# A graph network's second layer: ScalarE fetches one tile of rows in every 16 chunks, as SyncE does, in place of one in every 32

## The reference, cut to what matters

```python
h = jnp.maximum(_layernorm(x, axis=-1), 0.0)
H = jnp.einsum('ni,rio->rno', h, W)          # 8 relations
msg = (H[etype, src] + b[etype]) * norm
out = jax.ops.segment_sum(msg, dst, num_segments=h.shape[0])
x = x + jax.nn.relu(out)
```

## Time and profile before

| | us |
|---|---|
| median of 3 runs | 11777.57 (11773.84 to 11794.78) |
| the profiled execution | 11662.24 |
| its span, first to last instruction | 11659.8 |
| PE busy in the span | 7838.2 (67%) |
| POOL busy | 5846.3 (50%) |
| DVE busy | 4276.2 (37%) |
| ACT busy | 2363.0 (20%) |

### The profile page before, as it was taken

One profiled execution on the slowest core, in us unless ns is written; L12 is line 12 of the kernel. 1 busy time (PEld: TensorE's weight loads), 2 busy tenths in 40 slices (PEclk: granted clock), 3 DMA queues, 4 the chain that ended last, 5 costly groups with the idle time before them and its releaser, 6 DMA issues.

```text
span 11659.8 us, 215368 instructions
## 1 busy us (share of the span) xinstructions
PE 7838.2 (67%) x52954; PEld 6037.6 (52%) x52954; DVE 4276.2 (37%) x15012; ACT 2363.0 (20%) x7307; POOL 5846.3 (50%) x6213
## 2 busy tenths in 40 slices
PE   6777777777777777776555655655565555655555
PEld 5655566565665566565444444444444444444444
DVE  4333333333333333334333333333333333333333
ACT  4333333333333333334000000000000000000000
POOL 3555555555555555554444444444444444444444
PEclk8888888888888888888776777767767776777777
DMA  4222222222222222222111111111111111111111
GB/s 105 64 64 63 63 64 63 63 64 64 63 64 64 63 63 64 62 64 76 35 34 34 35 35 35 36 35 34 35 35 34 35 35 34 36 35 35 35 35 52
DMA packets 630303, 585.31 MB, mean 50 GB/s; under 512 B 306227, under 2 KB 505147, under 8 KB 629228
## 3 DMA queue, kind: packets, MB, share of 16 engines
q0 software_dynamic: 197856, 251.86, 9.9%
q1 hardware_dynamic: 422268, 325.27, 9.7%
q10 hardware_dynamic: 9600, 1.60, 0.1%
HBM read 558.88 MB, written 19.27 MB: 50 GB/s over the span
## 4 chain that ended last, share of the span: by engine, by line
SPq 31%; issue 21%; DVE 0%; PE 0%; DMA 0%; ACT 0%; DVEq 0%
SPq L548 26%; SPq L543 4%; SPq L448 1%; SPq L538 0%; SPq L555 0%; DVE res L1057 0%; SPq L414 0%; SPq L354 0%; PE bank L1222 0%; PE bank L1209 0%; DMA h_tab<-h_place 0%; PE bank L1255 0%; SPq L564 0%; DMA h_place<-in_src_t 0%; ACT h_place L660 0%
## 5 line engine op out<-in xcount | busy, mean ns | idle before, releaser
L617 POOL DMA_INDIRECT rows_place<-h_tab,idx x3055 | 2881.8, 943 | 3237.7 <-DMA idx<-in_src_t 1871.4
L617 POOL DMA_INDIRECT shared<-p_tab,idx x3128 | 2950.0, 943 | 2472.7 <-remote 992.1
L1209 PE MATMUL bank<-shared,rows_place 128*128 128x256 f32 x6110 | 2155.8, 508 | 902.4 <-DMA rows_place<-h_tab,idx 609.7
L1021 DVE SCALAR_TENSOR_TENSOR shared<-bank,key,late 128x256 f32<-128x256 f32 x3128 | 1280.3, 476 | 2932.8 <-remote 1843.2
L1209 PEld LDWEIGHTS bank<-shared,rows_place 128*128 128x128 f32 x6110 | 1490.7, 255 | 1286.0 <-DMA rows_place<-h_tab,idx 629.1
L1115 PE MATMUL bank<-h_sb,w_tile 128*128 128x128 f32 x6256 | 1079.3, 325 | 892.8 <-DVE h_sb L932 874.4
L1115 PEld LDWEIGHTS bank<-h_sb,w_tile 128*128 128x128 f32 x6256 | 909.8, 224 | 1105.0 <-DVE h_sb L932 1095.1
L775 ACT ACTIVATE h_place<-bank 128x256 f32<-128x256 f32 x782 | 298.7, 383 | 5773.2 <-remote 3342.2
L1222 PE MATMUL bank<-h_place,w_rel_sb 128*128 128x64 f32 x6256 | 915.2, 297 | 332.1 <-issue 331.4
L1134 PE MATMUL bank<-wn_half,h_sb 128*128 128x128 f32 x6256 | 1078.3, 326 | 0.0
L1222 PEld LDWEIGHTS bank<-h_place,w_rel_sb 128*128 128x128 f32 x6256 | 844.1, 212 | 348.6 <-issue 323.3
(11 more groups left out here) (94 smaller groups left out, 7034.4 us busy)
## 6 DMA issues: line engine op xcount, KB each, us to landing
rows_place<-in_dst_c SPq DMA_DIRECT2D x782, 192.0 KB
h_place<-h_tab SPq DMA_DIRECT2D x6272, 0.5 KB
shared<-in_edge_cols SPq DMA_DIRECT2D x782, 128.0 KB
shared<-p_tab,idx POOLq DMA_INDIRECT x3128
h_place<-h_tab ACTq DMA_DIRECT2D x3072, 0.5 KB
rows_place<-h_tab,idx POOLq DMA_INDIRECT x3055
qr_f<-qr_tab SPq DMA_DIRECT2D x782, 36.0 KB
idx<-in_src_t SPq DMA_DIRECT2D x393, 8.0 KB, 1.7
```

Source lines behind the costliest of these rows:

```text
L617: pool.indirect_dma_start(out=rows_of[s][:, t, :], out_offset=None, in_=table, in_offset=bass.IndirectOffsetOnAxis(ap=idx[k][:, s * TC + t ...
L1021: ins = dve.scalar_tensor_tensor(out=hot_rel[u % 2][:, t, :], in0=ps_key, scalar=key[k][:, n * TC + t:n * TC + t + 1], in1=w_f[:, ds(c.i * ...
L1209: pe.matmul(bank[s][:, 0:RW], there, hot_rel[s % 2][:, t, :], start=(t == 0), stop=(t == TC - 1))
```

## The change

ACT now fetches a tile of every superchunk, as SP does: SP fetches tile 0 of chunk 13 and ACT tile 1 of the same chunk. Both take 8 rows in each chunk's step. ACT begins two steps earlier than SP (`lead` 2), so that its last 8 rows are issued in its step of chunk 11 and SP's in the step of chunk 13. The number of ACT's tiles goes from 24 to 49 and of its rows from 3072 to 6272, and POOL gathers 3030 tiles in place of 3055. Chunk 15 is gathered whole. One load of 256 numbers by SP in step 5 brings both lists of a superchunk; ACT's own loads of lists are gone. ACT waits for that load in its step of chunk 12, and before its first copy of the layer it waits for the first list and issues 32 rows. SP issues the first list load once the last use of its place in the buffer has been stored, and waits for the other stores behind it. At chunk 13 PE waits for two semaphores, those of SP's rows and of ACT's.

```diff
-    ACT_ROWS = 5
-    ACT_FED_AT = SUP - 1
@@
-        fed_rows = h[2]
-        act_fed_rows = h[3][:, 2, :]
-        act_fed_ids = h[3][0:1, 3, :].bitcast(i32)
-        fed_ids = [h[3].rearrange("p j d -> p (j d)")[0:1, k * P:(k + 1) * P].bitcast(i32) for k in range(2)]
+        fed_rows = h[2][:, 0:4, :].rearrange("p (k f) d -> p k f d", f=2)
+        fed_ids = [h[3].rearrange("p j d -> p (j d)")[0:1, 2 * k * P:2 * (k + 1) * P].bitcast(i32) for k in range(2)]
@@
+        def feed(eng, f, lone, piece, landed):
+
+            _, at = nc.values_load_multi_w_load_instructions(
+                fed_ids[lone.half][0:1, f * P + piece * FED_ROWS:f * P + (piece + 1) * FED_ROWS], engines=(eng.engine,),
+                min_val=0, max_val=NPAD - 1, skip_runtime_bounds_check_because="a source node's number is below the number of nodes")
+            for k, row in enumerate(at):
+                p = piece * FED_ROWS + k
+                eng.dma_start(fed_rows[p:p + 1, lone.half, f, :], h_tab[ds(row, 1), :]).then_inc(landed[lone.half], 16)
+
+        def feed_step(eng, f, lead, u, lone, after, landed):
+
+            first = FED_AT - lead - SUP + 1
+            if u - first < SUP:
+                feed(eng, f, lone, u - first, landed)
+            elif after:
+                if u == first + SUP:
+                    eng.wait_ge(fed_ids_landed, 16 * after.ids_turn + 16)
+                    hold(eng)
+                feed(eng, f, after, u - first - SUP, landed)
+
+        def feed_first(eng, f, lead, m, landed):
+
+            eng.wait_ge(fed_ids_landed, 16 * Lone(m, 0, 0).ids_turn + 16)
+            hold(eng)
+            for piece in range(SUP - 1 - FED_AT + lead):
+                feed(eng, f, Lone(m, 0, 0), piece, landed)
@@
             def load_ids(lone):
-                sp.dma_start(fed_ids[lone.half], src_t[:, ds((lone.k * SUP + FED_AT) * TC, 1)].rearrange("p o -> o p"),
+                sp.dma_start(fed_ids[lone.half], src_t[:, ds((lone.k * SUP + FED_AT) * TC, 2)].rearrange("p o -> o p"),
@@
+                    feed_step(sp, 0, 0, u, lone, after, sp_row_landed)
@@
-                gather(c, k, two, h_tab, rows, scattered, idx1_landed, rows_landed, range(u == FED_AT or act_fed(u, lone), TC))
+                gather(c, k, two, h_tab, rows, scattered, idx1_landed, rows_landed, range(2 if u == FED_AT else 0, TC))
@@
             def copy_sums(c, u, k, two, lone, after):
...
+                feed_step(act, 1, 2, u, lone, after, act_row_landed)
@@
             with act.Fori(0, passes) as m:
+                feed_first(act, 1, 2, m, act_row_landed)
                 superchunks(act, m, copy_sums)
@@
                 if u == FED_AT:
-                    pe.wait_ge(fed_row_landed[lone.half], 16 * P * lone.turn + 16 * P)
-                if act_fed(u, lone):
-                    pe.wait_ge(act_row_landed, 16 * P * lone.act_turn + 16 * P)
+                    pe.wait_ge(sp_row_landed[lone.half], 16 * P * lone.turn + 16 * P)
+                    pe.wait_ge(act_row_landed[lone.half], 16 * P * lone.turn + 16 * P)
@@
-                    if u == FED_AT and t == 0:
-                        there = fed_rows[:, lone.half, :]
-                    if act_fed(u, lone) and t == 0:
-                        there = act_fed_rows
+                    there = fed_rows[:, lone.half, t, :] if u == FED_AT and t < 2 else rows[s][:, t, :]
```

More of the change, by code:

```diff
@@ L236, in gnn_two_layers @@
         pass1_ready, pass1_step = sem("pass1_ready"), sem("pass1_step")
-        fed_ids_landed, fed_row_landed = sem("fed_ids_landed"), slot_sems("fed_row_landed", 2)
-        act_ids_landed, act_row_landed = sem("act_ids_landed"), sem("act_row_landed")
+        fed_ids_landed = sem("fed_ids_landed")
+        sp_row_landed, act_row_landed = slot_sems("sp_row_landed", 2), slot_sems("act_row_landed", 2)
         block = ctx.enter_context(nc.Block())
@@ L344, in __init__ @@
             def __init__(self, m, two, half):
-                self.m, self.half, self.two = m, half, two
+                self.m, self.half = m, half
                 self.k = two * 2 + half
-                self.act_turn = m * (NSUP // 2) + two
                 self.turn = m * LONE_USES[half] + two
@@ L362, in superchunks @@
                 step(Chunk(m, quad, u % SL), u, quad % 2, m * (NQ // 2) + quad // 2, Lone(m, NSUP // 2, 0), None)
-        def act_fed(u, lone):
-            return u == ACT_FED_AT and lone.half == 1
         def tiles_gathered(c, u, lone):
-            if c.slot == ACT_FED_AT % SL:
-                return (c.m * (TC * SLOT_USES[c.slot] - NSUP // 2) + lone.two * (2 * TC * SUP // SL - 1)
-                        + (TC * ((lone.half * SUP + u) // SL + 1) - act_fed(u, lone)))
             if c.slot != FED_AT % SL:
                 return TC * c.turn + TC
-            return (c.m * (TC * SLOT_USES[c.slot] - (NSUP + 1)) + lone.k * (TC * SUP // SL - 1)
-                    + (TC * (u // SL + 1) - (u >= FED_AT)))
+            return (c.m * (TC * SLOT_USES[c.slot] - 2 * (NSUP + 1)) + lone.k * (TC * SUP // SL - 2)
+                    + (TC * (u // SL + 1) - 2 * (u >= FED_AT)))
+        def feed(eng, f, lone, piece, landed):
[19 more added lines that the diff above has]
+                feed(eng, f, Lone(m, 0, 0), piece, landed)
         def quads_after_first(eng, m, step):
@@ L532, in _ @@
             passes = number_of_passes(sp)
-            for k in range(HB):
-                sp.wait_ge(h_stored[k], 16 * ((NG - k + HB - 1) // HB))
             def load_ids(lone):
-                sp.dma_start(fed_ids[lone.half], src_t[:, ds((lone.k * SUP + FED_AT) * TC, 1)].rearrange("p o -> o p"),
+                sp.dma_start(fed_ids[lone.half], src_t[:, ds((lone.k * SUP + FED_AT) * TC, 2)].rearrange("p o -> o p"),
                              allow_slow_non_contiguous=True).then_inc(fed_ids_landed, 16)
[L541 to L548, removed]
             def layer1_pass(m):
-                FIRST = FED_AT - SUP + 1
                 def step(c, u, k, two, lone, after):
@@ L559, in step @@
                         load_ids(after)
[L560 to L566, removed]
+                    feed_step(sp, 0, 0, u, lone, after, sp_row_landed)
+                sp.wait_ge(h_stored[3], 16 * ((NG - 3 + HB - 1) // HB))
                 load_ids(Lone(m, 0, 0))
[L569 to L572, removed]
+                for k in range(3):
+                    sp.wait_ge(h_stored[k], 16 * ((NG - k + HB - 1) // HB))
+                feed_first(sp, 0, 0, m, sp_row_landed)
                 superchunks(sp, m, step)
@@ L758, in _ @@
                     normalise(NG + g - 1, g - 1)
[L761 to L768, removed]
             def copy_sums(c, u, k, two, lone, after):
```

1 line of the change is left out of this document (removed).

## The result

Six runs of each kernel: before 11781.43 us median (11773.84 to 11794.78), after 11851.97 us (11845.97 to 11866.21). The ratio is 1.0061 [1.0048, 1.0074]: 70.5 us slower, inside the range and 8 us from the forecast of 11860. The profiled execution took 11845.97 us. That of before was 1% under its own plain runs, so the 184 us between the two profiled executions are more than the change: SP's first list load of layer 2 comes at 5549.2 us where it came at 5507.7, and the only thing changed ahead of it is that it waits for three stores less, which can't make it later.

A forecast was written before the change was run, and what follows sets the result against it. SP's stream of single-row issues was taken to bound layer 2. Terms -22 (gathers), +18 (list), -2 (start) and +88 (ACT's rows) gave 82 us, added to 11777.57 for 11860 us; range 11700 to 12040, slower likeliest at 0.53.

The forecast's parts named there:

- What bounds the kernel: Layer 2 is as long as SP's stream of row issues, about 125 us a superchunk; POOL, PE, DVE, ACT have slack.
- A tile less for POOL: POOL's 25 fewer gathers in layer 2 each spare SP's stream 0.88 us: 22 us gained, bounds 0 and 31.
- A list of 256 numbers: SP's 49 longer list issues cost 0.38 us more each: 18 us lost, bounds 0 to 30.
- The start: SP's first list load of layer 2 no longer waits for three stores: 2 us gained, bounds 0 to 3.
- 3200 more rows on ACT: At chunk 13 PE waits for ACT's late tile, 1.8 us a superchunk: 88 us lost, bounds 0 and 294.
- The walk: One superchunk traced on ACT: its rows land at 8257 against 8262.12 for SP's, 5 us to spare, no cost.
- Rival 2: ACT's rows slow SP's row issues through one shared descriptor generator, 0.08 us a row, 256 us: 12028 us; chance 0.15.
- the two spacings: SP's list loads, 129.2 us apart with ACT issuing in all 16 steps, 122.5 with about 8: 0.17 us a row at most.
- Rival 1: ACT's 5 us to spare hold in every superchunk, only -6 us is left: 11772 us, no change; chance 0.22.
- Rival 3: A busier ACT breaks up POOL's bursts, so SP's rows go faster: 118 us gained, 11654 us; chance 0.25.
- the mark of the forecast: Between SP's list loads a superchunk would take about 126.7 us if ACT's tile lands just behind SP's.
- The rule on the descriptor generator: Skill's rule that the shared generator is locked per DMA instruction; the earlier trace shows no such ACT-SP cost where POOL rests.

The follow-up runs named there:

- no_feed: Kernel after with no single rows by SP or ACT, POOL gathering all 3128 tiles of layer 2: 10368.82 us, ratio 0.8798 to the kernel before.
- no_act: Kernel after without any rows by ACT, POOL gathering tiles 1 to 3 of chunk 13 (3079 gathers): 11479.62 us, ratio 0.9867 to the kernel before.
- act_unread: Kernel after with ACT's 6272 rows issued but unread, 3079 gathers by POOL, ACT itself waiting for their landing: 11793.98 us, ratio 1.0148 to the kernel before.

## Why the prediction was right, and for the wrong reason

- **What bounds the kernel** held: SP's row issues are the chain before and after, and no_feed shows that without them the lists come in time.
- **A tile less for POOL, -22 us.** The count was right, the price too high. By the table a gather costs SP 1.25 x (1 - 0.68 / 1.29) = 0.59 us, not 0.88, an estimate. I had priced an undisturbed row at 4.13 / 8 = 0.52 us from one stretch, where SP needs 0.69 at rest over the whole layer, and put all that SP lost beyond that down to POOL. ACT's part in it (1.17 to 1.29 us a row) is smaller: without it the price is 0.52. That makes -15 us.
- **A list of 256 numbers, +18 us.** The sign was right. The issue took 729 ns, 0.125 us more and not 0.38, so 6 us.
- **The start, -2 us.** Too small to be read between two executions that differ by 42 us ahead of layer 2.
- **3200 more rows on ACT, +88 us.** This step failed: "I take 1.8 us a superchunk" for a tile that lands behind SP's. The start of ACT's last issue is 7.4 us or more ahead of PE in all 49, that of SP's 1.47 on the mean, so the term is its own lower bound, 0. The walk had it right (5 us to spare, against 9.5 between the two last issues on the mean) and I overruled it without a row that spoke for 1.8. The walk itself was on the dear side: the rows of its ten steps took 31.2 us by ACT's timeline, 0.62 us each and not 0.78; the rest was waiting. By the prediction's own last sentence, that it is wrong if ACT's last rows are issued well ahead of SP's, its mechanism is refuted, though the time lies 8 us from the forecast.
- **Rival 2,** which had 0.15, is what happened: ACT's rows slow SP's stream. The runs no_act and act_unread settle it. I argued against it that the two spacings alternate with other things too, and looked at one pair. The pair was misread as well: 81 and 48 of ACT's rows lie in the two spacings, 33 rows apart and not 40. Over all the spacings between two list loads, but the first, the 24 with 78 of ACT's rows on the mean take 126.4 us and the 23 with 50 take 123.8: 0.09 us a row, a sign of rival 2 in the trace of before. Its size was 0.08 us a row; act_unread measured 0.050. From the result, 70.5 + 15 + 2 - 6 = 82 us stay for 3200 rows, 0.026 us each. So the sum met the result by luck: one term of about 80 us took the place of another, and it was the smaller end of rival 2 that made them alike.
- **Rival 1** fell by the ratio, 1.0061 [1.0048, 1.0074]. **Rival 3** fell: the spacing grew from 124.7 to 127.6 us. The 126.7 that I had given as the mark of the forecast (by the sum it is 124.7 + 82 / 49 = 126.4) could not tell it from a small rival 2; ACT's absence from the chain did.
- **The rule on the descriptor generator.** Where POOL rests, ACT's rows cost SP nothing (0.695 against 0.675 us), as the prediction said of the earlier trace rows. The Trainium skill, "Perfetto Trace Analysis", in its part on the DMA instruction of the hardware path, has the generator locked for one instruction at a time. A cost of such a lock that doesn't depend on POOL would show at rest too, and it doesn't; the cost is there only together with POOL's gathers, and only on chips 5 and 15 and that of the result. Against a lock as its cause is also that two thirds of the long instructions of SP's rows are register instructions, not DMA issues.

**What stays open.** What SP, ACT and POOL share during a burst: shown is only that ACT's work on rows matters, read or unread, and that chip 11 has none of it. What part of this work it is (issues, transfers, register instructions or their fetching) isn't shown, since the run with empty instructions doesn't have them in its trace. The rows' price isn't one number: act_unread and after differ by 49 gathers and ACT's wait, and their ratios by 0.0083 (98 us, from two chips), where 49 x 0.6 us = 29 us would be expected. It wasn't tried whether rows issued only in POOL's gaps are free with the tile in time, and no_feed wasn't run on the second kind; by the line of the gathers it would be some 8018 us there, an estimate, slower than both kernels.

## What to carry to other kernels

When an engine ends the chain with many short DMA issues, count them by what the other issuing engines do at that moment: giving a third engine part of the work can slow the one that ends the chain, though neither waits for the other. When a walk through the trace gives a bound and you take a value away from it, ask which other row would give the same time; two mechanisms with one spacing need a mark that tells them apart. Look in the trace of a control for what it was meant to add: empty instructions that aren't in the trace prove nothing. And before a change of some 0.5% is kept, run it on a second chip: here the same edit is 0.6% slower on one and 0.4% faster on another, as SP or POOL is in the chain.

## What the runs showed of the hardware

- Chips differ. The kernel before took 11627 and 11781 us on chips with a granted clock of 0.78, and 7925 us on one with 0.938. Layer 1, where SP issues no single rows, is shorter there too: SP's first row starts at 4072 us in place of 5554. Busy work is alike (a gather 943 and 944 ns); the rate at which SP and ACT get through their queues while POOL gathers isn't (1.17 to 1.47 us a row of SP against 0.60).
- On the first kind SP's stream has 4500 to 4900 pauses of some 0.70 us each, most of them beside POOL's gathers, on chip 11 none of this length. Single instructions of a row (even a register move) take up to 1.4 us in a burst of POOL, and 8 rows of ACT take 14.58 us, in place of 3.03 at rest. On the second, 8 rows of ACT take 3.03 to 3.34 us beside POOL's gathers.
- The issue of one DMA on SP takes 0.228 us for one row, 0.604 us for 128 numbers to one partition, and 0.729 us for 256.
